# Key and query features from folded weights, in a graph layer on one core

## The reference

```python
xn = _layernorm(x)
# 1. edges: 64 paths, each multiplies one 32-wide segment of x[src] with one of the edge row
contrib = path_coeffs * xn[src][:, i1, :] * edge[:, i2, :]     # summed by i3, then by dst
# 2. mixing: linear attention, 8 heads of 64
q, k, v = (xn @ W_qkv)                                         # 512 -> 3 x 512
q_prime = elu(q @ random_matrix) + 1                           # 64 -> 32 for each head
k_prime = elu(k @ random_matrix) + 1
kv = einsum('bshd,bshf->bhdf', k_prime, v)
z  = (q_prime @ kv) / (q_prime . sum(k_prime) + 1e-6)
x = x + edges + z @ W_out + b_out
# 3. experts: 2 shared and 64 routed SwiGLU blocks of 512x512, 6 of the 64 for each node
x = x + ffn(_layernorm(x))
```

## Time and profile before

| | us |
|---|---|
| median of 3 runs | 1029.3 |
| lowest, highest | 1023.42, 1030.47 |
| the profiled execution | 1017.46 |
| its span | 1015.7 |
| PE busy in the span | 907.1 |
| DVE busy | 548.3 |
| ACT busy, POOL busy | 255.0, 277.3 |

### The profile page before, as it was taken

How to read it: one execution, slowest core, us unless ns; L and a number is a source line. 1 busy time by engine, 2 the same in 40 slices (tenths; PEclk the granted TensorE clock), 3 DMA queues, 4 the chain that set the end, 5 groups by cost and what they waited for, 6 DMA issues and landing times.

```text
span 1015.7 us, 20874 instructions
## 1 busy us (share of the span) xinstructions
PE 907.1 (89%) x7513; PEld 588.4 (58%) x7513; DVE 548.3 (54%) x1623; ACT 255.0 (25%) x577; POOL 277.3 (27%) x265
## 2 busy tenths in 40 slices
PE   1699999998778298999999999999999999999991
PEld 1455555665544196676556666766676665656660
DVE  7598888989897986323324333334233333333216
ACT  3111110103122132332322223233332332323230
POOL 4436333434300102222222322222222332222111
PEclk9799999999999689999999999999999999999996
DMA  8834656555447942889979999999988999999976
GB/s 285 269 112 161 238 187 243 208 207 208 166 109 239 390 186 73 306 310 345 405 291 329 356 399 413 392 394 366 404 319 331 353 414 396 364 376 372 405 265 254
DMA packets 76931, 300.71 MB, mean 296 GB/s; under 512 B 13730, under 2 KB 14119, under 8 KB 58548
## 3 DMA queue, kind: packets, MB, share of 16 engines
q1 hardware_dynamic: 57256, 254.21, 65.9%
q0 software_dynamic: 17280, 38.48, 10.6%
q10 hardware_dynamic: 2252, 6.06, 1.6%
HBM read 290.26 MB, written 26.62 MB: 312 GB/s over the span
## 4 chain that ended last, share of the span: by engine, by line
PE 67%; DVE 10%; issue 7%; DMA 5%; DVEq 4%; POOL 3%; ACT 1%; another core or an unknown queue 1%; SPq 1%; ACTq 0%; POOLq 0%
PE bank L1826 23%; PE bank L1851 15%; DVE arena L1198 6%; PE bank L1791 5%; PE bank L1836 5%; PE bank L1675 5%; PE bank L1803 4%; PE bank L1815 3%; POOL arena L685 3%; DVEq L1196 2%; DMA arena<-in_L_mix_W_qkv_dram 2%; PE bank L1820 2%; PE bank L1584 2%; PE bank L1595 1%; DMA sums_d<-arena 1%
## 5 line engine op out<-in xcount | busy, mean ns | idle before, releaser
L1198 DVE TENSOR_TENSOR arena<-arena 128x288 f32 (+1 forms) x640 | 236.1, 443 | 30.8 <-remote 14.3
L1826 PE MATMUL bank<-arena,low 128*64 128x256 f32 x2048 | 241.6, 385 | 0.4 <-issue 0.4
L1826 PEld LDWEIGHTS bank<-arena,low 128*64 128x64 f32 x2048 | 139.8, 137 | 75.4 <-issue 12.5
L1675 PE MATMUL bank<-arena,multi 128*64 128x256 f32 x1296 | 157.6, 389 | 25.4 <-issue 14.9
L1851 PE MATMUL bank<-arena,low 128*64 128x256 f32 x1392 | 161.5, 379 | 1.4 <-ACT low L976 1.1
L741 POOL DMA_INDIRECT low<-xr_d,idx x64 | 90.7, 1418 | 235.6 <-DVE place L1431 177.0
L1675 PEld LDWEIGHTS bank<-arena,multi 128*64 128x64 f32 x1296 | 95.3, 139 | 85.3 <-issue 31.9
L745 POOL DMA_INDIRECT y_d<-low,place x64 | 68.3, 1067 | 262.9 <-ACT low L983 181.3
L1851 PEld LDWEIGHTS bank<-arena,low 128*64 128x64 f32 x1392 | 100.3, 137 | 51.9 <-ACT low L976 1.3
L685 POOL DMA_INDIRECT arena<-xn_d,ssel x79 | 98.8, 1251 | 42.9 <-issue 22.3
L983 ACT ACTIVATE low<-bank,gcol 64x256 f32<-64x256 f32 x174 | 81.6, 469 | 106.4 <-PE bank L1851 105.3
(11 more groups left out here) (214 smaller groups left out, 735.7 us busy)
## 6 DMA issues: line engine op xcount, KB each, us to landing
arena<-in_L_ffn_Wg_dram SPq DMA_DIRECT2D x64, 1024.0 KB
arena<-in_L_ffn_Wu_dram SPq DMA_DIRECT2D x64, 1024.0 KB
arena<-in_L_ffn_Wd_dram SPq DMA_DIRECT2D x64, 1024.0 KB
arena<-in_edge_attr_dram SPq DMA_DIRECT2D x88, 256.0 KB
arena<-y_d SPq DMA_DIRECT2D x5, 1250.0 KB, 7.7
sums_d<-arena ACTq DMA_DIRECT2D x18, 256.0 KB, 6.1
arena<-sums_d SPq DMA_DIRECT2D x4, 896.0 KB
arena<-in_L_mix_W_qkv_dram SPq DMA_DIRECT2D x2, 1024.0 KB, 19.2
```

The source lines that it names most:

```text
L1198: return dve.tensor_tensor(prod[:, buf, 0:n, EXT * p:EXT * p + EXT], x1[b][:, 0:n, bass.ds(i1, EXT)], x2[b][:, 0:n, bass.ds(i2, EXT)], ALU ...
L1675: ins = pe.matmul(bank[2 * b + c // 2][64 * h:64 * h + 64, 256 * (c % 2):256 * (c % 2) + 256], pair[:, pairs, i, :], prod[:, buf, i, 256 * ...
L1826: ins = pe.matmul(out_bank[64 * h:64 * h + 64, w * HF:(w + 1) * HF], xgT[:, b, k, 64 * o:64 * o + 64], gu[:, slot, w, k, h * HF:(h + 1) * HF],
```

## The change

- The four transposed 128-row parts of the key weights are formed on PE (`turn_weights`, after chunks 0 and 1), copied by ACT, and multiplied with the random matrix (`fold_weights`, after chunks 2 and 3): 512x256 folded weights `wR`. `k_features` then multiplies the nodes with `wR` directly. The same for the queries after chunks 18 to 21, and `q_features` after 22 and 23. `project_k` and `project_q` are gone.
- `turn_ends(1)` comes first on PE, ahead of the waits for the key weights and the transposed nodes; no projection is left ahead of chunk 0.
- `keys_values` moves from chunks 22 to 25 to 14 to 17, `mix_values` from 28, 29, 32, 33, 36 to 24, 25, 28, 29, 32, `z_transpose` from 31, 32, 35, 36, 38 to 27, 28, 31, 32, 34. The last `normalize` moves from chunk 38, after 12 products, to chunk 33, after 6.
- The query weights are loaded in the block of window 4 instead of 3, after a wait for the last `k_features`.

```diff
-        MIXED = (31, 32, 35, 36, 38)
+        MIX = (24, 25, 28, 29, 32)
+        MIXED = (27, 28, 31, 32, 34)
...
-                if w == 3:
-                    sp.wait_ge(s_kp, 8)
+                if w == 4:
+                    sp.wait_ge(s_kfp, TT)
                     sp.dma_start(wq, w_tiles[:, :, 0:D]).then_inc(s_wq, 16)
...
+            def take_turned(i, turned, taken):
+                act.wait_ge(turned, i + 1)
+                act.copy(wT[:, i, :], bank[4 + i][:, :]).then_inc(taken, 1)
+
+            def take_folded(i, folded, taken):
+                act.wait_ge(folded, DC + i + 1)
+                act.copy(wR[:, 2 * i:2 * i + 2, :], bank[4 + i][:, :].rearrange("p (c n) -> p c n", c=2)).then_inc(taken, 1)
...
-                    if k + 1 in MIXED[0:4] and p == 6:
+                    if k + 1 in MIXED and p == 6:
                         normalize(MIXED.index(k + 1))
-                    if k == 38 and p == 12:
-                        normalize(TT - 1)
...
+            def turn_weights(w, i, turned):
+                for c in range(DC):
+                    ins = pe.transpose(bank[4 + i][:, c * 128:(c + 1) * 128], w[:, c, i * 128:(i + 1) * 128], ident[:, :])
+                ins.then_inc(turned, 1)
+
+            def fold_weights(i, taken, folded):
+                pe.wait_ge(s_rm, 32)
+                pe.wait_ge(taken, DC)
+                for j in range(2):
+                    for c in range(DC):
+                        ins = pe.matmul(bank[4 + i][:, 256 * j + 64 * c:256 * j + 64 * c + 64], wT[:, c, (2 * i + j) * 128:(2 * i + j + 1) * 128],
+                                        rm2, start=True, stop=True)
+                ins.then_inc(folded, 1)
...
-                for c in range(4):
-                    ins = pe.matmul(bank[6 + t % 2][0:TR, 64 * c:64 * c + 64], kT[:, c, t * TR:(t + 1) * TR], rm2, start=True, stop=True)
+                for c in range(DC):
+                    ins = pe.matmul(bank[6 + t % 2][0:TR, 0:256], xT[:, c, t * TR:(t + 1) * TR], wR[:, c, :],
+                                    start=(c == 0), stop=(c == DC - 1))
                 ins.then_inc(s_kfp, 1)
...
-                for hp in range(2):
-                    ins = pe.matmul(bank[4 + u][64 * hp:64 * hp + 64, 0:n], rm2, qT[:, 2 * g + hp, a:a + n], start=True, stop=True)
+                for c in range(DC):
+                    ins = pe.matmul(bank[4 + u][:, 0:n], wR[:, c, 128 * g:128 * g + 128], xT[:, c, a:a + n],
+                                    start=(c == 0), stop=(c == DC - 1))
                 ins.then_inc(s_qfp, 1)
...
-            pe.wait_ge(s_wk, 16)
-            pe.wait_ge(s_xT, TT)
-            project_k(0)
             pe.wait_ge(s_choose, 3)
             turn_ends(1, bank[1])
-            for u in range(1, 4):
-                project_k(u)
             pe.wait_ge(s_iota, 2)
+            pe.wait_ge(s_xT, TT)
 
             for k in range(HOT):
                 window_chunk(k)
-                if k <= 3:
-                    project_k(k + 4)
+                if k in (0, 1):
+                    if k == 0:
+                        pe.wait_ge(s_wk, 16)
+                    turn_weights(wk, 2 * k, s_kp)
+                    turn_weights(wk, 2 * k + 1, s_kp)
+                if k in (2, 3):
+                    fold_weights(k - 2, s_kT, s_kp)
...
-                if 14 <= k <= 21:
-                    project_q(k - 14)
-                if 22 <= k <= 25:
-                    keys_values((k - 22) // 2, *((0, 3), (3, TT))[k % 2])
-                if k in (26, 27):
-                    q_features(2 * k - 52)
-                    q_features(2 * k - 51)
-                if k in (28, 29, 32, 33, 36):
-                    mix_values((28, 29, 32, 33, 36).index(k))
+                if 14 <= k <= 17:
+                    keys_values((k - 14) // 2, *((0, 3), (3, TT))[k % 2])
+                if k in (18, 19):
+                    if k == 18:
+                        pe.wait_ge(s_wq, 48)
+                    if k == 19:
+                        pe.wait_ge(s_kv, 2)
+                    turn_weights(wq, 2 * k - 36, s_qp)
+                    turn_weights(wq, 2 * k - 35, s_qp)
+                if k in (20, 21):
+                    fold_weights(k - 20, s_qT, s_qp)
+                if k in (22, 23):
+                    q_features(2 * k - 44)
+                    q_features(2 * k - 43)
+                if k in MIX:
+                    mix_values(MIX.index(k))
```

More of the change, by code:

```diff
@@ L192, in gps_layer @@
         prod, x1, x2, stage, sums, pair = m["prod"], m["x1"], m["x2"], m["stage"], m["sums"], m["pair"]
-        wk, wv, wq, kT, v, z, zT, qp, kp, kvm, xo = (m[k] for k in ("wk", "wv", "wq", "kT", "v", "z", "zT", "qp", "kp",
-                                                                          "kvm", "xo"))
-        qT, wout_sb, rm2, acc, bias = kT, m["wout"], m["rm2"], m["acc"], m["bias"]
+        wk, wv, wq, wT, wR, v, z, zT, qp, kp, kvm, xo = (m[k] for k in ("wk", "wv", "wq", "wT", "wr", "v", "z", "zT", "qp", "kp",
+                                                                              "kvm", "xo"))
+        wout_sb, rm2, acc, bias = m["wout"], m["rm2"], m["acc"], m["bias"]
         gu, dn, shgu, shdn, terms, total = m["gu"], m["dn"], m["shgu"], m["shdn"], m["terms"], m["total"]
@@ L901, in start_acc @@
                 ins.then_inc(s_zeroed, 1)
-            for u in range(4):
-                take_k(u)
             for k in range(HOT):
@@ L911, in _ @@
                     flush(k // CHUNKS)
-                if k <= 3:
-                    take_k(k + 4)
+                if k in (0, 1):
+                    take_turned(2 * k, s_kp, s_kT)
+                    take_turned(2 * k + 1, s_kp, s_kT)
+                if k in (2, 3):
+                    take_folded(k - 2, s_kp, s_kT)
                 if k in (4, 6, 8, 10, 12):
@@ L1577, in _ @@
                 ins.then_inc(s_xTp, 1)
[L1579 to L1586, removed]
+            def turn_weights(w, i, turned):
[10 more added lines that the diff above has]
+                ins.then_inc(folded, 1)
             def project_v(t):
                 if t == 0:
-                    pe.wait_ge(s_kT, 8)
+                    pe.wait_ge(s_kT, DC + 2)
                     pe.wait_ge(s_wv, 16)
@@ L1619, in keys_values @@
                     ins.then_inc(s_kvp, 1)
[L1621 to L1630, removed]
-                    ins = pe.matmul(bank[4 + u % 4][:, 0:n], wq[:, k, c * 128:(c + 1) * 128], xT[:, k, a:a + n],
-                                    start=(k == 0), stop=(k == DC - 1))
-                ins.then_inc(s_qp, 1)
             def q_features(u):
                 g, (a, n) = u // 2, HALVES[u % 2]
-                pe.wait_ge(s_qT, 8)
-                if u >= 2:
-                    pe.wait_ge(s_kv, u - 1)
-                for hp in range(2):
-                    ins = pe.matmul(bank[4 + u][64 * hp:64 * hp + 64, 0:n], rm2, qT[:, 2 * g + hp, a:a + n], start=True, stop=True)
+                pe.wait_ge(s_qT, DC + 2)
+                for c in range(DC):
+                    ins = pe.matmul(bank[4 + u][:, 0:n], wR[:, c, 128 * g:128 * g + 128], xT[:, c, a:a + n],
+                                    start=(c == 0), stop=(c == DC - 1))
                 ins.then_inc(s_qfp, 1)
```

34 lines of the change are left out of this document (15 added, 19 removed).

## The result

The changed kernel took 1017.0 us (median of 15 runs, 1013.8 to 1022.1) where the kernel before took 1026.9 on the same chip (15 runs): a ratio of 0.991, with an interval of 0.989 to 0.993, so 9.3 us less (7.5 to 11.1). The forecast was 8.1 us less, and for the time 1012 to 1029.

What follows compares the result with a forecast made beforehand. DVE was taken to pace the edge loop, with PE work between chunks worth at most 3.5 us. -9.3 - 0.4 + 1.0 + 0.5 + 3.2 - 3.1 = -8.1 us, carried to the median as 1021.2; range 1012 to 1029.

Steps and rivals of the forecast that it cites:

- start: Ahead of the edge loop: ends turned at once, so the first product starts at 29.3 instead of 38.64; -9.3 us.
- window 0: Chunks 0 and 1: DVE's waits for PE go, -1.0, against chunk 0 slow on an idle PE; together -0.4 us.
- key features, windows 2 and 3: Wider `k_features`, five times +1.0 on PE, which catches DVE around chunks 11 to 15: +1.0 us, 0 to 3.0.
- queries (wait in chunk 25): `q_features` grows to 4.6 us after chunks 22 and 23; DVE has 1.4 us of room: +0.5, 0 to 2.5.
- new wait, with the normalising: Chunk 33: DVE waits 2.8 us for the fifth tile's mixing, plus 0.4 normalising ahead of chunk 35: +3.2 us.
- end: Behind chunk 35: clearing runs beside the chunk, the store is issued 3.4 us earlier; -3.1, between -3.4 and 0.
- (d): Rival at the start: folded weights do nothing for time and the edge rows bind; inside the range (-7.8), no chance given.
- the 7.8: Gain at the start if window 0's edge rows came only with the key weights, first product at about 30.8.
- the store has its own turn: At the loop's end: DMA engines go round-robin over queues, so the store isn't held behind the loads; -3.1 stands, not 0.
- (b): Rival: the end gives nothing, store lands with the loads, PE shows 2 us more at the features; -3, 1026, chance 0.17.
- rival (a): The start without the givebacks, PE having more room or POOL's 3.7 not recurring: -13 to -15, 1015, chance 0.2.
- rival (c): Gaps on PE hold its clock at 1.2 GHz through chunks 18 to 21: +12 us, 1041, chance 0.05.

Runs made afterwards that it cites:

- after_ctl2: Changed kernel with one register instruction more ahead of eight waits in the expert part, second set: 1016.1 us, 0.998 of the plain kernel before, 0.994 of its own baseline.
- before_ctl: Kernel before with the same register instruction more ahead of eight waits, baseline of the second set: 1020.3 us, 1.004 of the plain kernel before.
- after_ctl3: Changed kernel with the register instruction, third set: 1016.6 us, 1.000 of the plain kernel before, 0.996 of its own baseline.
- before_ctl2: Kernel before with the register instruction, baseline of the third set: 1021.3 us, 1.004 of the plain kernel before.
- norm_later: Changed kernel with register instruction, fifth tile transposed after chunk 36 and normalised in 35 instead of 34 and 33: 999.2 us, 0.996 against the control's 1.001.
- clear_late: Changed kernel with register instruction, ACT's clearing held until chunk 35 has left PE: 1004.9 us, 1.003 against the control's 1.001.
- start_alone2: Kernel before with register instruction, second window's ends turned first and the first projection moved behind chunk 0: 1017.3 us, 0.996 of its own baseline.
- set 3: Third set of four kernels on one chip, 5 rounds each, with the plain kernel before, which took 1016.5 us.
- kf_half: Changed kernel with register instruction, key features summed over half the inputs: 1023.1 us, 1.005, not comparable because routing differs; only the loop can be compared.
- sets 2 and 3: Second and third sets of four kernels, each on one chip, 5 rounds each; the plain kernel before took 1017.8 and 1016.5 us.
- spread: Changed kernel with register instruction, one `q_features` piece after each of chunks 22 to 25, mixing and normalising later: 1010.5 us, 0.989 of its own baseline.
- set 1: First set of four kernels on one chip, 5 rounds each, with the plain kernel before, which took 1002.5 us.

## Why the prediction was right, and where it was not

The total was right on the chip where it was measured: -9.3 against a forecast of -8.1, and 1017.0 in a range of 1012 to 1029. On the two others, by their own baselines, it was -5.9 and -4.6. Why the first chip showed more stays open: its one trace of after holds more givebacks than the others, and a time of 1019.6. So the closeness of the total is in part luck. Two of the prediction's own signs went against it: the path sums were to start at 311.3 instead of 319.4 and started at 321.33, and waits for PE were to stay under 5 us in the loop where the trace of after names PE for 4.3 + 4.1 + 0.6 = 9.0. The terms, as differences between two traces each: after less before, `after_ctl2` less `before_ctl`, `after_ctl3` less `before_ctl2`:

| step | forecast | measured, three pairs |
|---|---|---|
| start | -9.3 | -8.8, -8.7, -8.8 |
| window 0 | -0.4 | -0.4, +0.1, -1.0 |
| key features, windows 2 and 3 | +1.0 | +5.6, +1.0, +1.1 |
| unnamed wait of chunk 17 | 0 | +3.7, +2.2, +2.9 |
| queries (wait in chunk 25) | +0.5 | +3.0, +3.5, +3.6 |
| new wait, with the normalising | +3.2 | +4.5, +2.4, +3.0 |
| end | -3.1 | -3.3, -2.1, -3.1 |

The rows leave out window 1 and the windows 5 and 7; the path sums moved by +1.9, -0.9 and -3.3 in all. In the first pair 3.0 of the 5.6 us is chunk 9, which waits 5.07 instead of 2.05, while window 1 is 2.0 us shorter, mostly because POOL's 3.7 is missing; and 3.2 is chunk 15, with the slow step ahead of it.

**Right**: the start. ACT's square root and not the edge rows held the first product, within 0.5 us of the forecast, so (d) and the 7.8 fell. The new wait, its place, its cause and that it was paid in full (`norm_later`). The end, and with it the argument that the store has its own turn (`clear_late`); (b) fell. Also that the removed PE work ahead of the loop is worth only what DVE waits for: `start_alone2` keeps all of it and waits 3.4 us for it.

**Mis-sized**: the queries, +0.5. The sum for PE was close: on a chip without unnamed waits DVE waited 2.45 for chunk 24, the upper end of my range. Where there are such waits I had let DVE's longest one (3.6) cover PE's lateness. The runs show the opposite. I had read the 14.3 us "to a queue without a name" as DVE losing time to something other than PE. They are waits for PE's chunks whose semaphore updates come late, counted from the end of the chunk, so whatever PE is late is added to them and not hidden in them: in chunk 25 the wait is 6.3, with PE 2 us further behind than before and the update 1.5 later. The same holds at the key features, where the wait of chunk 17 went from 2.1 to 5.0 in set 3 (PE 1.8 further behind, the update 1.1 later). I had taken +1.0 and missed the 2.9 behind it. Together the two were about 6 us too small in set 3, and the rival (a), with no givebacks at all, was the wrong way to widen the range. The bound that work taken off PE between chunks is worth at most 3.5 us rests on the same reading. It was not tested on the kernel before; in the changed one `kf_half` took out 4.3 us and moved the path sums by 5.5.

**The clock**, rival (c), did not occur as a loss. Rows of PE's chunks 18 and 19 in the kernel after, as a timeline:

```profile
171.11 4.11 PE L1667 MATMUL bank<-arena,multi 128*64 128x256 f32 x36 [0.35 <-DVE arena L1202]
175.15 1.09 PE L1583 MATMUL bank<-ident,arena 128*128 128x128 f32 x8
177.19 4.11 PE L1667 MATMUL bank<-arena,multi 128*64 128x256 f32 x36 [0.96 <-DVE arena L1202]
```

They take 4.11 each at full clock. In the repeats of sets 2 and 3 chunk 20, the third of the four, was slow (5.79 in `after_ctl2` after an idle 2.10), and DVE did not wait for it. Other chunks ran partly at 1.2 GHz too, and one of them, 32, stands on the critical path: of the 4.11 us of the new wait 1.7 are the 5.79 it took instead of 4.11. The row of PE's granted clock on the page, one digit for each fortieth of the span, has the dip of the start (second digit) and that of 280 to 305 us (twelfth, with chunks 33 to 35; the granted clock from 284 to 290 us is 0.51). From 153 to 280 us, where chunks 18 to 21 lie, it stays at 9, although it was 0.72 from 272 to 278 us, beside chunk 32: a slice of 25 us hides a short dip.

```profile
PEclk9699999999989789999999999999999999999996
```

## What to carry to other kernels

Idle time of the engine that doesn't pace is the room for a moved step, and a step of twice the size needs it in one place: the same four pieces of `q_features` cost 3.6 us in chunk 25 as two pairs and nothing one behind each chunk (`spread`). When a step moves to an earlier chunk, move its consumer by no more than that: the fifth tile's mixing came four chunks earlier and its normalising more than five, and the lost distance became a wait of 2 to 4 us on the engine that paces. Before a wait that the profile doesn't name is counted as another's, look up which semaphore the waiting line waits for, and when the engine behind it was done. And take the baseline with every helper that the experiments need: one register instruction ahead of eight waits cost 4 us, half of the effect.

## What the runs showed of the hardware

The kernel before took 1002.5 us (median) on the chip of set 1, and 1016.5, 1017.8 and 1026.9 in the other three comparisons. On the fast one DVE had no unnamed wait in the loop (four kernels were traced there, this one not); in the three traces of the kernel before there were 7 of 1.3 to 3.6 us, 14 in all, one a window. They are waits for a PE chunk that has ended: its semaphore update came 1.9 to 4.8 us behind the chunk's last matmul, where on the fast chip it came 0.02 to 0.03 behind. ACT, which waits for the same chunk, mostly starts within 0.3 us of DVE. PE runs on: `q_features` took its usual 4.47 us in the middle of such a wait, though some chunks of the time have pauses of up to 1.2 us. In the changed kernel the lateness is up to 6.9 us. What makes it stays open; moving 1 MB of weight loads away did not touch it (4.91 in chunk 17).

PE's clock isn't foretold by the idle time ahead alone. Chunks after idle 2.10 (chunk 20 of `after_ctl2`), 2.56, 2.82 and 2.96 us took 5.79, one after 2.55 and one after 3.25 (at 237.1 in the kernel after) took 4.11.
